# Start of a perceiver layer in float32 halves: TensorE begins with products of zeros, the first K product runs by chunk over four PSUM banks, and four steps change places

## What is computed

```python
x = x + xattn(layernorm(x), ctx, mask, Wq, bq, Wkv, bkv, Wo, bo)   # 16 heads of 32, rotary q and k
x = x + attn(layernorm(x), ...)                                    # causal self-attention, 16 heads
x = x + ffn(layernorm(x), gate_w, gate_b, expert_w, expert_b)      # 8 experts, the best 2 of each row
```

## Time and profile before

| | us |
|---|---|
| runs of the kernel before | 857.13, 857.54, 847.47 (median 857.13) |
| profiled execution | 847.62 |
| its span, first to last instruction | 845.8 |
| TensorE busy | 770.9 (91%) |
| DVE, ACT, GpSimd busy | 458.9, 342.1, 235.7 |
| mean granted clock of TensorE | 0.951 |

### The profile page before, as it was taken

The page is one execution under the profiler, slowest core; times in us unless marked ns, Lnnn a source line. Parts: engine busy times, 40 slices in busy tenths (PEclk is TensorE's granted clock), DMA queues, the critical chain, the costliest instruction groups (busy, mean ns, idle before and its releaser), DMA issues. The chain is left out here.

```text
span 845.8 us, 21194 instructions
## 1 busy us (share of the span) xinstructions
PE 770.9 (91%) x8896; PEld 642.7 (76%) x8897; DVE 458.9 (54%) x991; ACT 342.1 (40%) x807; POOL 235.7 (28%) x200
## 2 busy tenths in 40 slices
PE   5999999999999999999999999997999971699990
PEld 4788888888889888888888888865777750477770
DVE  4745464564555554554545547565766668921114
ACT  5433533444335334443353354334444464123330
POOL 1241223113212321231122122313222308345540
PEclk9999999999999999999999999998999975679995
DMA  9621011001000100010011002028000000034438
GB/s 301 235 81 72 27 34 45 27 27 52 27 27 27 52 27 27 27 52 26 28 43 35 27 28 94 12 87 361 15 24 12 26 26 13 11 115 160 151 124 310
DMA packets 18788, 61.16 MB, mean 72 GB/s; under 512 B 2824, under 2 KB 3208, under 8 KB 16784
## 3 DMA queue, kind: packets, MB, share of 16 engines
q1 hardware_dynamic: 15024, 47.87, 16.0%
q0 software_dynamic: 3680, 12.06, 4.3%
HBM read 49.70 MB, written 10.23 MB: 71 GB/s over the span
## 5 line engine op out<-in xcount | busy, mean ns | idle before, releaser
L152 PE MATMUL bank<-chi,wparts 128*128 128x258 f32 x512 | 150.1, 293 | 8.1 <-DVE wparts L608 8.0
L153 PE MATMUL bank<-clo,wparts 128*128 128x258 f32 x512 | 145.9, 285 | 0.0
L154 PE MATMUL bank<-chi,wparts 128*128 128x258 f32 x512 | 145.8, 285 | 0.0
L152 PEld LDWEIGHTS bank<-chi,wparts 128*128 128x128 f32 x512 | 97.8, 191 | 21.1 <-issue 12.8
L313 POOL TENSOR_TENSOR ksin<-kb,const 128x1032 f32<-128x1032 f32 x32 | 95.3, 2978 | 64.2 <-ACT kb L372 64.2
L729 PE MATMUL bank<-wparts,chi 128*128 128x512 f32 x256 | 105.6, 413 | 0.2 <-DVE wparts L591 0.2
L319 POOL TENSOR_TENSOR pdiag<-pr,const 128x128 f32<-128x128 f32 x32 | 13.0, 407 | 330.2 <-ACT pr L380 330.2
L730 PE MATMUL bank<-wparts,chi 128*128 128x512 f32 x256 | 101.5, 396 | 0.0
L731 PE MATMUL bank<-wparts,clo 128*128 128x512 f32 x256 | 101.3, 396 | 0.0
L154 PEld LDWEIGHTS bank<-chi,wparts 128*128 128x128 f32 x512 | 98.4, 192 | 0.0
L153 PEld LDWEIGHTS bank<-clo,wparts 128*128 128x128 f32 x512 | 98.3, 192 | 0.0
(11 more groups left out here) (235 smaller groups left out, 1629.2 us busy)
## 6 DMA issues: line engine op xcount, KB each, us to landing
craw<-ctx_t_dram SPq DMA_DIRECT2D x32, 516.0 KB, 3.4
expert_lo<-weights_dram SPq DMA_DIRECT2D x8, 1024.0 KB, 12.4
wraw<-weights_dram SPq DMA_DIRECT2D x7, 1024.0 KB, 6.7
expert_lo<-ffn_out_scratch SPq DMA_DIRECT2D x16, 256.0 KB, 5.1
x<-x_dram SPq DMA_DIRECT2D x8, 256.0 KB, 7.3
ffn_xn_scratch<-xn SPq DMA_DIRECT2D x8, 256.0 KB, 2.0
out_dram<-x SPq DMA_DIRECT2D x8, 256.0 KB, 4.7
wraw<-weights_dram SPq DMA_DIRECT2D x4, 256.0 KB, 6.2
```

The lines of the kernel that those rows point to most:

```text
L152: pe.matmul(psum, ahi(c), bhi(c), start=(c == 0), stop=False)
L153: pe.matmul(psum, ahi(c), blo(c), start=False, stop=False)
L154: last = pe.matmul(psum, alo(c), bhi(c), start=False, stop=(c == chunks - 1))
```

## The change

1. DVE first fills `kcos` (128 x 4 x 258 elements) with zeros. TensorE then does eight products of 128 x 128 with 128 x 256 of it, in plain float32, into the first score bank; nobody reads the result.
2. The first K product is issued chunk by chunk: in each chunk all four K products, in banks 0, 1, 2 and in `score[1]` (the first bank of `quad`), instead of one K product after the other.
3. ACT's x parts move ahead of the q weight chunks; on DVE the x low part moves ahead of the q weight low parts.
4. SP issues the V weights ahead of the q bias row.
5. On DVE `q_rope(0)` moves ahead of `k_cos(0)`.
6. The q product and the first V product of the opening wait for each weight chunk instead of the whole; each low chunk signals.
7. TensorE does V product 1 ahead of the transposes of q.

```diff
@@ -210,6 +210,7 @@
             proj = bank[0:3]
             score = [bank[3], quad[:, 0, :], quad[:, 1, :], quad[:, 2, :]]
             extra = score[3]
+            first_k = [*proj, score[1]]
             av = quad[:, 3, 0:P]
             spread = quad[:, 3, P:3 * P]
 
@@ -264,8 +265,8 @@
                 sp.dma_start(bias_cols[:], bias_cols_in).then_inc(s_biask, 16)
                 sp.dma_start(const[:], const_in).then_inc(s_const, 16)
                 weight(WQ)
+                weight(WV)
                 bias_row(R_BQ, s_bq)
-                weight(WV)
                 ctx(1, 1)
                 bias_row(R_BV, s_bv)
                 sp.dma_start(maskb8[:, 0:BT, :], mask_in[0:BT].partition_broadcast(P)).then_inc(s_maskin, 16)
@@ -369,7 +370,8 @@
                     if m == 0 and not at_start(b):
                         act.wait_ge(s_kcos, b)
                         act.wait_ge(s_ksin, b)
-                    act.activation(kb[:, m, :], proj[m % 3][:, 0:LKP], ACT.Identity,
+                    psum = first_k[m] if at_start(b) else proj[m % 3]
+                    act.activation(kb[:, m, :], psum[:, 0:LKP], ACT.Identity,
                                    bias=bias_cols[:, m:m + 1]).then_inc(s_kev, 1)
 
                 def exp(b, g):
@@ -424,10 +426,10 @@
                     act.activation(whi[WK][:, c, :], wraw[0][:, c, :], ACT.Copy).then_inc(s_wkhi, 1)
                 act.wait_ge(s_biask, 16)
                 k_evac(0, 0)
+                xt_hi(0)
                 w_hi_chunks(WQ)
                 for m in range(1, 4):
                     k_evac(0, m)
-                xt_hi(0)
                 w_hi_chunks(WV)
                 ctx_hi_at(0, 1)
                 act.wait_ge(s_maskin, 16)
@@ -588,9 +590,8 @@
                             dve.wait_ge(s_whi_chunk, (n - WQ) * (KC - 1) + c + 1)
                         else:
                             dve.wait_ge(s_whi, n)
-                        lo = dve.tensor_tensor(wlo[n][:, c, :], wraw[n % 2][:, c, :], whi[n][:, c, :].bitcast(F32),
-                                               ALU.subtract)
-                    lo.then_inc(s_wlo, 1)
+                        dve.tensor_tensor(wlo[n][:, c, :], wraw[n % 2][:, c, :], whi[n][:, c, :].bitcast(F32),
+                                          ALU.subtract).then_inc(s_wlo if c == KC - 1 else s_wklo, 1)
 
                 def v_last():
                     dve.wait_ge(s_vl, 1)
@@ -602,21 +603,22 @@
                     dve.wait_ge(s_vlsb, 1)
                     dve.tensor_tensor(vlast[:], sums[:, :, 1, :], vlast[:], ALU.add).then_inc(s_vlsb, 1)
 
+                dve.memset(kcos[:], 0.0).then_inc(s_zero, 1)
                 ctx_lo(0, 0)
                 for c in range(KC):
                     dve.wait_ge(s_wkhi, c + 1)
                     dve.tensor_tensor(wlo[WK][:, c, :], wraw[0][:, c, :], whi[WK][:, c, :].bitcast(F32),
                                       ALU.subtract).then_inc(s_wklo, 1)
                 dve.wait_ge(s_x0, 16)
-                dve.wait_ge(s_zero, 1)
+                dve.wait_ge(s_zero, 2)
                 ln(0, x[:, 0, :])
-                w_lo_chunks(WQ)
                 dve.wait_ge(s_const, 16)
                 xt_lo(0)
+                w_lo_chunks(WQ)
                 w_lo_chunks(WV)
-                k_cos(0)
                 dve.wait_ge(s_bq, 16)
                 q_rope(0)
+                k_cos(0)
                 ctx_lo(1, 1)
                 dve.wait_ge(s_bv, 16)
                 v_evac(0, 0, 0)
@@ -686,12 +688,19 @@
                         last = pe.transpose(extra[:, c * P:(c + 1) * P], xn[:, c * P:(c + 1) * P], ident)
                     last.then_inc(s_xtp, 1)
 
+                def weight_chunk(n, c):
+                    if c == KC - 1:
+                        pe.wait_ge(s_wlo, n)
+                    else:
+                        pe.wait_ge(s_wklo, KC + (n - WQ) * (KC - 1) + c + 1)
+
                 def q_product(t, b=None):
                     pe.wait_ge(s_xtlo, t + 1)
                     if b is not None:
                         pe.wait_ge(s_pt, (b + 1) * G)
                     mm3(pe, extra, lambda c: xthi[:, c, :], lambda c: xtlo[:, c, :],
-                        lambda c: whi[WQ][:, c, :], lambda c: wlo[WQ][:, c, :]).then_inc(s_qmm, 1)
+                        lambda c: whi[WQ][:, c, :], lambda c: wlo[WQ][:, c, :],
+                        before=(lambda c: weight_chunk(WQ, c)) if at_start(t) else None).then_inc(s_qmm, 1)
 
                 def q_transposed(t, b=None):
                     pe.wait_ge(s_qr, t + 1)
@@ -702,29 +711,44 @@
                             last = pe.transpose(score[2 + i][:, g * P:(g + 1) * P], a[:, g * P:(g + 1) * P], ident)
                     last.then_inc(s_qtp, 1)
 
-                def wk_chunk(c):
-                    pe.wait_ge(s_wklo, c + 1)
+                def warm_up():
+                    pe.wait_ge(s_zero, 2)
+                    for i in range(8):
+                        pe.matmul(score[0][:, 0:2 * P], kcos[:, 0, 0:P], kcos[:, 1, 0:2 * P], start=True, stop=True)
+
+                def first_k_product():
+                    pe.wait_ge(s_clo, 1)
+                    for c in range(KC):
+                        pe.wait_ge(s_wklo, c + 1)
+                        for m in range(4):
+                            psum = first_k[m][:, 0:LKP]
+                            hi, lo = (a[:, c, m * P:(m + 1) * P] for a in (whi[WK], wlo[WK]))
+                            pe.matmul(psum, hi, chi[0][:, c, :], start=(c == 0), stop=False)
+                            pe.matmul(psum, hi, clo[0][:, c, :], start=False, stop=False)
+                            last = pe.matmul(psum, lo, chi[0][:, c, :], start=False, stop=(c == KC - 1))
+                            if c == KC - 1:
+                                last.then_inc(s_proj, 1)
 
                 def k_product(b, j, m):
                     if m == 0:
                         pe.wait_ge(s_clo, b + 1)
-                    if not (at_start(b) and m < 3):
-                        if m == 0:
-                            pe.wait_ge(s_kev, b * 4)
-                        elif m < 3:
-                            pe.wait_ge(s_vev, b * 2 - 2 + m)
-                        else:
-                            pe.wait_ge(s_kev, b * 4 + 1)
+                    if m == 0:
+                        pe.wait_ge(s_kev, b * 4)
+                    elif m < 3:
+                        pe.wait_ge(s_vev, b * 2 - 2 + m)
+                    else:
+                        pe.wait_ge(s_kev, b * 4 + 1)
                     mm3(pe, proj[m % 3][:, 0:LKP],
                         lambda c: whi[WK][:, c, m * P:(m + 1) * P], lambda c: wlo[WK][:, c, m * P:(m + 1) * P],
-                        lambda c: chi[j % 2][:, c, :], lambda c: clo[j % 2][:, c, :],
-                        before=wk_chunk if at_start(b) and m == 0 else None).then_inc(s_proj, 1)
+                        lambda c: chi[j % 2][:, c, :], lambda c: clo[j % 2][:, c, :]).then_inc(s_proj, 1)
 
                 def v_product(b, j, u):
 
                     psum = proj[(4 + u) % 3][:]
                     pe.wait_ge(s_kev, b * 4 + 2 + u)
                     for c in range(KC):
+                        if at_start(b) and u == 0:
+                            weight_chunk(WV, c)
                         hi, lo = (a[j % 2][:, c, u * P:(u + 1) * P] for a in (chi, clo))
                         pe.matmul(psum, hi, whi[WV][:, c, :], start=(c == 0), stop=False)
                         pe.matmul(psum, hi, wlo[WV][:, c, :], start=False, stop=False)
@@ -805,16 +829,14 @@
                     mm3(pe, extra, lambda c: othi[:, c, :], lambda c: otlo[:, c, :],
                         lambda c: whi[WO][:, c, :], lambda c: wlo[WO][:, c, :]).then_inc(s_wo, 1)
 
-                for m in range(4):
-                    k_product(0, 0, m)
+                warm_up()
+                first_k_product()
                 pe.wait_ge(s_const, 16)
                 xn_transposed(0)
-                pe.wait_ge(s_wlo, WQ)
                 q_product(0)
-                pe.wait_ge(s_wlo, WV)
                 v_product(0, 0, 0)
+                v_product(0, 0, 1)
                 q_transposed(0)
-                v_product(0, 0, 1)
 
                 def extra_free(t, j, first, last):
 
```

## The result

| | us |
|---|---|
| after, 22 runs | 857.02 median (854.7 to 858.64) |
| before, 22 runs beside them | 849.42 median (844.68 to 857.54) |
| ratio after / before | 1.0073, 95% interval 1.0053 to 1.0094 |
| profiled execution after | span 853.4 (before 845.8) |

The change made the kernel 0.7% slower, within 2% but clear of its interval, where 1.1 us faster was forecast. Of the 22 runs of before, 8 lie between 854.8 and 857.5 and 14 between 844.7 and 850.7; all 22 of after lie in the upper range. The change removed the lower level.

A forecast was written before the change was run, and what follows sets the result against it. TensorE, with transfers, was taken to bound the opening; the long middle is TensorE without a gap. Scores 2.65 us sooner, cut to 1.1 by the third context tile and last-row subtraction: 857.13 - 1.1 = 856.0 us, range 844.0 to 858.5.

The forecast's parts named there:

- What is late next: Fourth K product to last-row product: 2.1 us sooner at the first, 1.1 us at the second, after DVE's subtraction.
- the cap makes the forecast robust: Any first scores up to 30.1 us give the same 1.1 us gain, so a late clock or the memset changes nothing.
- the cap: Third context tile, converted by ACT at 32.35, limits the gain: 2.65 us at the scores becomes 1.1 us.
- nothing in the profile explains the upper: Runs before form two levels 9.7 us apart, unexplained; the 1.1 us was taken off the median, 857.13.
- The gain at the scores: End of the opening: first scores at 28.55 instead of 31.20, 2.65 us sooner.
- number 1: Third context tile lands earlier or waits behind it are shorter: the whole 2.65 us stays, 854.5 us; chance 20%.
- number 4: Clock does not fall at the last-row product as it did at 46 us: a further 1.75 us gained, 854.3; 10%.
- Number 3: Clock falls in the new wait before the q product: 856.0 to 857.1 us; chance 10%.
- The rule weighed for it: Wait before q, 2.1 us, plus four transposes could count as one idle stretch and drop the clock; the trace spoke against.
- Number 2: Opening: zeros do not raise the clock and only delay K; scores 0.9 us later, 858.0 us; chance 15%.

The follow-up runs named there:

- the yardstick: The changed kernel with both halves of the last context rows made in the opening, no wait added: 845.89 us, ratio to before 0.9928.
- experiment 1: The changed kernel, with GpSimd's output-weight low part also waiting until DVE has made the last context row's low part: 849.5 us.

## Why the prediction was wrong

The step that failed is in "What is late next": "now it runs 39.66 to 41.0. TensorE goes on at 41.05". It put the end of the layer norm at 39.64, where it was 41.58 (held by k_sin), and carried the subtraction's 1.36 us over from the row of before as if it were its length. That duration was a wait: for k_sin's end, in a stretch that GpSimd's next long operation had not yet reached. The prediction called the row "long for its 128 elements", bounded it below by nothing and above not at all, and never asked where GpSimd's 5 us operation would stand once ACT had released it 2 us sooner. Measured: 41.50 to 46.08. With it fell "the cap makes the forecast robust": a gain of the opening could now turn into a loss.

Right, by steps: the zeros ran from 1.99 (forecast 1.95) to 7.25 (8.1, at the lower bound of 7.2); K's end 13.78 (13.9); first scores 29.04 (28.55), the V chunks taking 4.10 instead of 3.37; tile converted at 32.50 (before 32.35) and the fourth K product 34.97 (34.95).

Two more steps were wrong in kind. The tile was called the cap; the yardstick with the tile early (845.88 against 845.89) shows that it is none where it usually lands. Its landing does matter, as the other runner in the race, and as a cap where it is late (experiment 1). And "nothing in the profile explains the upper" level: the profile had it, 0.6 us between the end of ACT's conversion and of k_sin, and 5 us of GpSimd behind. The forecast put the median of before on the upper level and took 1.1 off; the true median of before was on the lower, and 857.02 is the change's. The gain at the scores, 2.65 us, was a matter of size: it was counted from a profile in which the clock rose late, and against the five profiles of that opening the six of the new one have 1.6. That 856.0 lies 1.0 from the measured median, and within the stated range, is luck: a level that the forecast did not explain stood in for a loss that it did not see.

The rivals: number 1, the tile as no cap, was right of the tile, and its gain was lost at the subtraction all the same; number 4 had the place (the last-row product) and the wrong sign. Number 3 feared the new wait before q, 2.17 us. In the profile of after the clock held there. The rule weighed for it (The Trainium skill, TensorE: Matmul & The Clock Gate, "Part 4: PE-mode transpose"), that a transpose does not count as busy in the way a product does, left room for a fall. There was none: products of q behind the four transposes and the wait were 0.23 us apart. But in six of the eight profiles with this wait it did fall in the q product. The yardstick's:

```profile
17.29 0.39 PE L154 MATMUL quad<-wparts,xtlo 128*128 128x512 f32 x1
17.52 0.46 PE L152 MATMUL quad<-wparts,xthi 128*128 128x512 f32 x1
...
18.20 0.63 PE L154 MATMUL quad<-wparts,xtlo 128*128 128x512 f32 x1
18.63 0.63 PE L152 MATMUL quad<-wparts,xthi 128*128 128x512 f32 x1
```

From 0.23 the distance goes to 0.43, and the granted clock is 0.50 from 18 to 21 us. With zeros alone it fell as well, after a wait of 2.30 us. None of the five with the old wait of 1.6 us has such a fall. So the rival's event came in most profiles, though not in the one of the changed kernel, and cost nothing: the first scores follow K's end by the same 15.2 to 15.3 us with it and without, as the q product is over before the last V chunk (made by 22.84 in the profile of after). No run tells the transposes from the longer wait as its cause. What cost time was the fall in the 5.8 us wait, which no rival named. Number 2 falls by the spacing of 0.12 at 8.17 and by the run without zeros.

What stays open: what the zeros and the chunk order are each worth, as one profile a kernel cannot tell their gain from the changing moments at which the clock moves. Between 40 and 52 us it fell in 13 of the 14 profiles (0.50 from 44 in that of the kernel before with the last rows made early) and stayed at 1.00 in the yardstick's. Open too is why the changed kernel has all of its 22 runs on the upper level: the runs show that the race decides, and that an earlier tile wins it, but not which of the seven steps made it a sure loss.

## What to carry to other kernels

Before speeding one chain up, look at what each engine that it releases will start sooner, and at what shares a port with that. If a row is several times longer than the same shape elsewhere, its duration is a wait and must not be carried over: find whose end it ends with. When the runs of a kernel form two levels, look for two chains that finish within a microsecond of each other; taking the small operation out of the race (here into an idle stretch of the opening) was worth 2.1 us in the kernel before (847.64 against 849.71) and about 11 in the changed one (845.89 against 857.02, measured at different times), whose own 1.75 showed only then. And where the clock's rise moves by two us from run to run, a lead is not counted from one profile.

## What the runs showed of the hardware that was not expected

A 128 x 128 subtraction on DVE took 0.28 us alone, 1.36 behind k_sin and 4.58 behind a 128 x 2048 one on GpSimd; the two long ones each ended 0.15 us after GpSimd's operation. Products whose operands are all zero raised TensorE's clock to 2.4 GHz as others do: 16 records in 5.26 us and K products 0.12 us apart from 8.17; without them the products were 0.21 apart until 10.4. DVE's memset of 1032 float32 elements took 0.92 us, a little under the prediction's 1.1, which was also its estimate by the page that it names; the measurement decides.
